# A sorted segment sum and three-layer MLP on TensorE: even edge groups summed into the accumulating bank, odd ones into a staging bank

## The chip, the cores and the metric

One core of a Trainium2 chip. The metric is the device time of one execution in microseconds (us), the median over the runs of a kernel. All durations below are from one profiled execution of the kernel before, whose own time stands beside the others.

## The reference, cut to what matters

```python
def _L0_gnn_ref(x, edge_attr, edge_index, W1, b1, W2, b2, W3, b3):
    agg_edge = jax.ops.segment_sum(edge_attr, edge_index[1], num_segments=12500)
    collected = jnp.concatenate([x, agg_edge], axis=1)
    h = jax.nn.silu(collected @ W1 + b1)
    h = jax.nn.silu(h @ W2 + b2)
    return x + h @ W3 + b3          # OUT_DIM is the whole of x here

h = jnp.maximum(_layernorm(x, axis=-1), 0.0)
x = x + _L0_gnn_ref(h, edge_attr_48, jnp.stack([src, dst]), W1, b1, W2, b2, W3, b3)
```

x is 12500 x 128, edge_attr_48 is 200000 x 48, both f32; `dst` is sorted. W1 is 176 x 256, W2 256 x 256, W3 256 x 128.

## The kernel before, in words

**Groups, windows, tiles.** The edges are cut into NG = 391 groups of 512 (128 partitions times PER = 4). As `dst` is sorted and a node has 16 edges on average, the 512 edges of a group reach nodes within a window of WINDOW = 42 columns. VectorE compares the edges' relative targets with the 42 columns (`onehot_of`, L628 to L635), TensorE multiplies a group's edges (128 x 48, stationary) by its one-hot (128 x 42, moving), four times, one for each j. That is the group's sum. A tile is 448 nodes and, on average, GPT = 14 groups; there are NT = 28 tiles. A batch is the 14 groups of a tile, in two halves of seven that are loaded and turned to one-hots apart.

**Two steps for a sum.** `sum_tile` (L919 to L944) takes the groups in pairs. The even group of a pair goes to partitions 0 to 47 of the PSUM bank `stage` and the odd one to partitions 64 to 111 of it, by the two column halves of the array (`tile_position` (0, 0) and (0, 64)), in turn; all addresses are constants. ScalarE copies `stage` to SBUF (`stage_sums`, L437). `place_batch` (L946 to L959) then multiplies each staged window by a slice of the identity, and adds it into one of the two banks of `agg_ps` at the window's offset. This offset is known on the chip only: `offsets_of` (L908 to L914) loads the 14 offsets of a batch from SBUF into registers of TensorE's sequencer. A tile's bank gets groups from up to EARLY = 3 before to 3 after its own, so the batch that is placed is shifted by three groups against the one that is summed (`batch_of`, L901). Every f32 matmul runs as two passes, each with a weight load, so a batch of 14 groups has 112 passes in the sum and 28 in the placement.

**The pipeline.** Each engine has a queue of its own, worked in order, with semaphores between them; the order is written out by hand in a function `step(i, parity)` for each engine, with i = 1 to 29, of which 4 to 21 are a loop of two steps a turn (`pipeline`, L258). On TensorE (L1019) step i is: `layer1(i-1)`, `offsets_of(i+1)`, `sum_tile(i+1)`, `layer3(i-2)`, `transposes(i)`, `place_batch(i+1)`, `layer2(i-1)`. On VectorE (L827): `add_x` (L801), `carry_over` (L763, reads the tile's bank and carries its 64 columns of overhang), `relu_lo`, `agg_lo`, a one-hot half, the statistics of x of tile i+1, `add_b3`, the low parts of h1, the other one-hot half, `shift_of_norm` and `finish(i-2)` (L819, waits for layer 3). On ScalarE (L506): `relu`, `split_agg` (L481), `clear_bank` (L418), `activate2(i-2)` (L487, its two halves free the banks that `layer1` writes), `activate1`, `normalize(i)`, `stage_sums(i+1)`. SyncE issues all loads and stores; the load of x of tile i+1 waits for `add_x(i-1)`.

**Ahead of the steps.** TensorE turns four sets of rows for the relative targets and offsets (`turn_rows`), sums batches 0 and 1, transposes tile 0, loads two sets of offsets, looks at a flag that sends bad data to a general path (`where_invalid`, L268), places both batches. ScalarE zeroes `agg_carry` in three pieces (`clear_carry`, L426) and splits the weights.

Of the kernel before, what the change touches and what calls it, by code (L numbers as in the profile page):

```python
# [33 lines left out]
def gnn_kernel(nc, x, dst, edge_attr, W1, b1, W2, b2, W3, b3, out):  # L34
# [33 lines left out]
    STAGED = PAIRS * WINDOW  # L68
    assert WINDOW <= OVER and FULL_ROWS == ROWS - 1
# [5 lines left out]
    def groups_of(i, half):  # L75
# [8 lines left out]
    with ExitStack() as ctx:  # L84
# [40 lines left out]
        offset_row = sb("offset_row", [1, NT * SLOT], I32)  # L125
# [160 lines left out]
        def _(sp):  # L286
# [5 lines left out]
            def load_edges(i, parity, half):  # L292
                n, full = groups_of(i, half)
# [3 lines left out]
                e0 = (i * GPT + half * HALF) * GROUP  # L297
                sp.dma_start(raw[:, slot, 0:full].rearrange("p g j d -> p g (j d)"),
                             edge_attr[bass.ds(e0, full * GROUP), :].rearrange(
# [66 lines left out]
            def step(i, parity):  # L366
                if has(i, -1, NT):
                    load_x(i + 1, 1 - parity)
                for half in range(2):
                    if has(i, -3, NT):  # L370
# [11 lines left out]
        def _(pool):  # L382
# [12 lines left out]
            pool.memset(w1e_lo[:, :].bitcast(F32), 0.0).then_inc(s_pool_zero, 1)  # L395
            pool.memset(agg_carry[:, 0:POOL_ZEROS], 0.0).then_inc(s_carry0, 1)
# [20 lines left out]
        def _(act):  # L417
# [19 lines left out]
            def stage_sums(t, parity):  # L437

                act.wait_ge(s_summed, 2 * t + 2)
                if not isinstance(t, int) or t > 1:  # L440
                    act.wait_ge(s_placed, t)
                act.activation(staged[:, parity].rearrange("d k w -> d (k w)"), stage[0:ROW2 + ED, 0:STAGED],
                               ACT.Copy).then_inc(s_staged, 1)
# [5 lines left out]
            rel_of(0)  # L449
            stage_sums(0, 0)  # L450
            clear_carry(1)
# [54 lines left out]
            def step(i, parity):  # L506
                if has(i, 1, NT):
                    relu(i - 1)
                if isinstance(i, int) and i == 1:
                    clear_carry(2)  # L510
# [19 lines left out]
        def _(dve):  # L530
# [97 lines left out]
            def onehot_of(i, parity, half):  # L628
                n, _ = groups_of(i, half)
                slot = 2 * parity + half  # L630
                cols = rel[:, :, :].rearrange("p g j -> p (g j)")[
                    :, bass.ds((i * GPT + half * HALF) * PER, n * PER)]
                return dve.tensor_tensor(onehot[:, slot, 0:n * PER, :],  # L633
                                         window[:, :].unsqueeze(1).broadcast_to([P, n * PER, WINDOW]),
                                         cols.unsqueeze(2).broadcast_to([P, n * PER, WINDOW]), ALU.is_equal)  # L635
# [7 lines left out]
            def weights_lo():  # L643
                dve.wait_ge(s_w_hi, 4)
                dve.wait_ge(s_pool_zero, 4)
# [10 lines left out]
            def offsets_into(b, first, last, many=1):  # L656
                g0 = b * GPT - EARLY + first
# [4 lines left out]
            FULL0 = (P + EARLY) // GPT  # L662
            REST0 = (P + EARLY) % GPT
            offsets_into(0, EARLY, GPT)
# [24 lines left out]
            offsets_into(FULL0 + 1, 0, GPT, NT - 2 - FULL0)  # L689
            offsets_into(NT - 1, 0, NG + EARLY - (NT - 1) * GPT)  # L690
            dve.tensor_reduce(any_invalid[:, :], invalid_sum, AX.X, ALU.max).then_inc(s_off, 1)
            weights_lo()
            dve.wait_ge(s_rel, ROWS)
            load_stats(1, 1)
            dve.wait_ge(s_stats, 2)
            aggregate_stats(1, 1)
            for half in range(2):
                make_onehot(2, 0, half)
            shift_of_norm(1, 1)

            def general_path():
# [25 lines left out]
                dve.wait_ge(s_pool_zero, 4)  # L727
# [5 lines left out]
                dve.wait_ge(s_onehot, 6)  # L733
# [29 lines left out]
            def carry_over(t, parity):  # L763

                n = PER * nodes_p(t)
                if isinstance(t, int) and t == NT - 1:
                    dve.wait_ge(s_placed, NT)
                else:
                    dve.wait_ge(s_closed, t + 1)
# [57 lines left out]
            def step(i, parity):  # L827
                if has(i, 1, NT):
                    add_x(i - 1, 1 - parity)
# [3 lines left out]
                if has(i, -2, NT):  # L833
# [21 lines left out]
        def _(pe):  # L855
# [45 lines left out]
            def batch_of(b):  # L901

                t = isinstance(b, int)
                first = 0 if t and b == 0 else -EARLY
                last = sum(groups_of(b, half)[0] for half in range(2)) if t and b == NT - 1 else GPT - EARLY
                return first, last

            def offsets_of(b):  # L908
                first, last = batch_of(b)
                _, offsets = nc.values_load_multi_w_load_instructions(  # L910
                    offset_row[0:1, bass.ds(b * SLOT + (first + EARLY), last - first)], engines=[mybir.EngineType.PE],
# [7 lines left out]
            def sum_tile(i, parity):  # L919

                counts = [groups_of(i, half) for half in range(2)]
                total = sum(n for n, _ in counts)
                wait(pe, s_staged, i)
                for pair in range(PAIRS):
                    for k in (2 * pair, 2 * pair + 1):
                        n, full = counts[k // HALF]
                        slot = 2 * parity + k // HALF
                        if k % HALF == 0:
                            pe.wait_ge(s_edges[slot], 16 * slot_turn(i, parity) + (16 if full < n else 0))
# [150 lines left out]
```

## Time and profile before

| | us |
|---|---|
| median of 3 runs | 358.68 (357.7 to 360.31) |
| the profiled execution | 358.91 |
| its span | 357.1 |
| around the span | 1.8 |
| granted TensorE clock, mean over the span | 0.981 of full speed |

PE is TensorE's matmuls, PEld its weight loads, PEldq its sequencer (registers, semaphores), DVE VectorE, ACT ScalarE. A row of a timeline has the start in us from the span's start, the duration in us, the engine, line and operation, and in brackets the idle time of the engine before it and what ended that.

### The profile page before, as it was taken

What the parts mean: (1) busy time and instruction counts of PE and PEld (TensorE: products, weight loads), DVE (VectorE), ACT (ScalarE), POOL (GpSimd) and SP (SyncE); (2) the same over time, 40 slices, a digit from 0 to 9 for tenths busy, and PEclk for the clock granted to TensorE, in tenths of its full rate; (3) what the DMA queues carried; (4) which work ended last, traced back from release to release, by engine and by line L of the source; (5) the groups of instructions that cost most, each with busy time, mean ns of one, the idle gap of its engine ahead of it and who ended that gap; (6) DMA issues with size and microseconds to landing.
All of it is one profiled execution on the core that took longest, in us unless ns stands there. A gap on an engine that the chain in (4) does not pass through costs nothing.

```text
span 357.1 us, 13469 instructions
## 1 busy us (share of the span) xinstructions
PE 326.2 (91%) x5150; PEld 296.9 (83%) x5151; DVE 266.5 (75%) x638; ACT 214.4 (60%) x406; POOL 42.4 (12%) x44
## 2 busy tenths in 40 slices
PE   6654999999999999999999999999999999999985
PEld 5643888988898888988898889888898889888984
DVE  7881968978877797778777787879777877776462
ACT  8452675557656675567555765667555755567471
POOL 3041101111001110111001110111011101111000
PEclk9986799999999999999999999999999999999999
DMA  6984057733675356634674357534763456512111
GB/s 196 303 219 149 21 163 209 207 117 106 195 206 154 99 157 206 191 108 119 199 206 135 100 176 206 175 103 133 205 206 110 125 181 207 163 33 52 28 28 49
DMA packets 79194, 53.07 MB, mean 149 GB/s; under 512 B 2912, under 2 KB 78778, under 8 KB 79168
## 3 DMA queue, kind: packets, MB, share of 16 engines
q1 hardware_dynamic: 79168, 52.70, 51.2%
q8 instruction: 19, 0.31, 0.4%
q14 instruction: 7, 0.06, 0.1%
HBM read 46.29 MB, written 6.40 MB: 148 GB/s over the span
## 4 chain that ended last, share of the span: by engine, by line
PE 87%; issue 5%; ACT 4%; DVE 3%; POOL 0%; ACTq 0%; POOLq 0%; DVEq 0%
PE stage L937 21%; PE z L1015 15%; PE agg_ps L954 11%; PE z L1000 8%; PE z L1004 6%; PE z L1001 6%; PE z L983 3%; PE z L988 3%; PE z L984 3%; PE z L989 3%; PE z L985 3%; PE tp L967 3%; ACT xn L471 1%; ACT agg_carry L428 1%; DVE g_tilet L545 1%
## 5 line engine op out<-in xcount | busy, mean ns | idle before, releaser
L937 PEld LDWEIGHTS stage<-onehot,raw 128*48 128x48 f32 x3128 | 73.9, 126 | 19.7 <-issue 19.5
L937 PE MATMUL stage<-onehot,raw 128*48 128x42 f32 x3128 | 77.0, 215 | 10.0 <-issue 9.1
L633 DVE TENSOR_TENSOR onehot<-window,rel 128x1176 f32<-128x1176 f32 (+1 forms) x56 | 76.9, 1376 | 1.9 <-ACT rel L434 1.2
L403 POOL TENSOR_TENSOR rstd<-vareps,minus_half 112x4 f32<-112x4 f32 (+1 forms) x28 | 39.2, 1401 | 287.1 <-DVE vareps L617 287.1
L1015 PE MATMUL z<-w,h 128*112 128x128 f32 (+1 forms) x448 | 56.3, 278 | 1.4 <-ACT h L492 0.8
L1015 PEld LDWEIGHTS z<-w,h 128*112 128x112 f32 (+1 forms) x448 | 50.6, 176 | 3.4 <-issue 2.1
L824 DVE TENSOR_TENSOR out_t<-z,resid 112x512 f32<-112x512 f32 (+1 forms) x28 | 19.3, 691 | 41.5 <-PE z L1015 41.5
L492 ACT ACTIVATE h<-z,b2c 128x448 f32<-128x448 f32 (+1 forms) x56 | 35.4, 632 | 21.5 <-PE z L1004 20.3
L954 PE MATMUL agg_ps<-staged,ident 112*48 112x42 f32 x782 | 42.5, 219 | 4.8 <-issue 4.8
L954 PEld LDWEIGHTS agg_ps<-staged,ident 112*48 112x48 f32 x782 | 39.2, 129 | 8.7 <-issue 5.0
L479 ACT ACTIVATE hT_hi<-tp 128x448 fp32r<-128x448 f32 (+1 forms) x28 | 15.2, 542 | 51.6 <-PE tp L967 51.6
L471 ACT ACTIVATE xn<-x_t,nmr,rstd 112x128 f32<-112x128 f32 (+1 forms) x112 | 45.8, 479 | 0.0
L1000 PE MATMUL z<-h_hi,w_hi 128*128 128x448 f32 (+1 forms) x112 | 43.8, 391 | 0.0
L500 ACT ACTIVATE h<-z,b1c 128x448 f32<-128x448 f32 (+1 forms) x56 | 35.0, 625 | 12.8 <-PE z L989 12.8
L1001 PE MATMUL z<-h_hi,w_lo 128*128 128x448 f32 (+1 forms) x112 | 40.9, 365 | 0.0
L607 DVE BATCH_NORM_STATS2 stats<-x_t 112x6 f32<-112x128 f32 (+1 forms) x112 | 24.4, 280 | 20.8 <-DMA x_t<-in_x_dram 20.7
L798 DVE TENSOR_TENSOR h_lo<-h,h_hi 128x448 fp32r<-128x448 f32 (+1 forms) x56 | 33.2, 622 | 7.2 <-ACT h_hi L504 6.9
L485 ACT ACTIVATE agg_hilo<-agg 48x448 fp32r<-48x448 f32 (+1 forms) x28 | 16.2, 578 | 34.7 <-DVE agg L774 34.6
L504 ACT ACTIVATE h_hi<-h 128x448 fp32r<-128x448 f32 (+1 forms) x56 | 32.3, 576 | 1.8
L1004 PE MATMUL z<-h_lo,w_hi 128*128 128x448 f32 (+1 forms) x112 | 31.9, 366 | 0.0
L1000 PEld LDWEIGHTS z<-h_hi,w_hi 128*128 128x128 f32 x112 | 21.0, 187 | 2.6
L1004 PEld LDWEIGHTS z<-h_lo,w_hi 128*128 128x128 f32 x112 | 21.0, 188 | 1.8
(107 smaller groups left out, 404.7 us busy)
## 6 DMA issues: line engine op xcount, KB each, us to landing
raw<-in_edge_attr_dram SPq DMA_DIRECT2D x55, 672.0 KB, 5.5
x_t<-in_x_dram SPq DMA_DIRECT2D x27, 224.0 KB, 3.5
out_dram<-out_t SPq DMA_DIRECT2D x27, 224.0 KB, 3.6
dst_rows<-in_dst_dram SPq DMA_DIRECT2D x1, 512.0 KB
raw<-in_edge_attr_dram SPq DMA_DIRECT2D x1, 480.0 KB, 4.9
dst_rows<-in_dst_dram SPq DMA_DIRECT2D x1, 256.0 KB, 2.7
out_t<-in_L_gnn_W_dram SPq DMA_DIRECT2D x1, 256.0 KB, 8.1
x_t<-in_x_dram SPq DMA_DIRECT2D x1, 192.0 KB
```

Of the source, the lines that this page charges most:

```text
L403: pool.tensor_tensor(rstd[0:np_, parity], vareps[0:np_, :], minus_half[0:np_, :], ALU.pow).then_inc(s_rstd, 1)
L471: ln = act.activation(xn[0:np_, parity, q, :], x_t[0:np_, parity, q, :], ACT.Identity, bias=nmr[0:np_, parity, q:q + 1], scale=rstd[0:np_, ...
L492: act.activation(h2[:, m, 0:n], z[:, m, 0:n], ACT.Silu, bias=b2c[:, m:m + 1]).then_inc(s_h2, 1)
L500: act.activation(h1[:, m, 0:n], z[:, m, 0:n], ACT.Silu, bias=b1c[:, m:m + 1]).then_inc(s_h1, 1)
L633: return dve.tensor_tensor(onehot[:, slot, 0:n * PER, :], window[:, :].unsqueeze(1).broadcast_to([P, n * PER, WINDOW]), cols.unsqueeze(2). ...
L798: dve.tensor_tensor(h1_lo[:, m, 0:n], h1[:, m, 0:n], h1_hi[:, m, 0:n].bitcast(F32), ALU.subtract).then_inc(s_h1_lo, 1)
L937: mm = pe.matmul(stage[at:at + ED, pair * WINDOW:(pair + 1) * WINDOW], raw[0:rows, 2 * parity + half, k, j, :], onehot[0:rows, 2 * parity ...
L954: mm = pe.matmul(banks[0:ED, bass.ds(offset, WINDOW)], ident[0:ROW2 + ED, at:at + ED], staged[:, parity if k >= 0 else 1 - parity, group / ...
L1000: pe.matmul(z[:, m, 0:n], w2_hi[:, k, cols], h1_hi[:, k, 0:n], start=(k == 0), stop=False)
L1001: pe.matmul(z[:, m, 0:n], w2_lo[:, k, cols], h1_hi[:, k, 0:n], start=False, stop=False)
L1004: mm = pe.matmul(z[:, m, 0:n], w2_hi[:, k, cols], h1_lo[:, k, 0:n], start=False, stop=(k == M - 1))
L1015: mm = pe.matmul(z3[0:np_, q, :], h2[:, k, q * np_:(q + 1) * np_], w3[:, k, :], start=(k == 0), stop=(k == M - 1))
```

## The change

Batches are shifted by SHIFT = 4 groups, for the sum as for the placement, so batch b is the groups 14b-4 to 14b+9, batch 0 has 10 groups, and there is a batch 28 of 3 groups (NB = 29). In a pair the even group is summed by its four matmuls straight into `agg_ps` at its offset, while the odd group goes to `stage` as before; only the odd ones are staged and placed, 7 a batch. `sum_tile` so waits for the clear bank and needs the offsets. TensorE's step is turned: `layer2(i-2)` stands first, with the load of the offsets of batch i+1 between its two halves m. ScalarE copies 48 partitions in place of 112; rows 0 to 63 of `staged` are zeroed once by GpSimd. Prologue: the offsets of batch 0 are loaded before its sum, batch 0 is placed early, those of batch 1 are loaded ahead of the small matmuls, the general path's flag is read before the transposes; ScalarE zeroes the second piece of `agg_carry` before it stages batch 0; VectorE moves the second half of one-hot 2, `shift_of_norm(1)` and `add_x(0)` behind the first `carry_over`, `relu_lo` and `agg_lo`. The last tile is normalized one step earlier.

```diff
     def groups_of(b, half):
-        g0 = i * GPT + half * HALF if isinstance(i, int) else 0
-        n = min(HALF, NG - g0)
-        return n, min(n, NG - 1 - g0)
+        g0 = b * GPT - SHIFT + half * HALF
+        if not isinstance(b, int):
+            return g0, 0, HALF, HALF
+        at = max(0, -g0)
+        n = max(0, min(HALF, NG - g0))
+        return g0 + at, at, n, min(n, max(at, NG - 1 - g0))
@@ stage_sums (ScalarE)
-                if not isinstance(t, int) or t > 1:
-                    act.wait_ge(s_placed, t)
-                act.activation(staged[:, parity]..., stage[0:ROW2 + ED, 0:STAGED],
+                wait(act, s_placed, t - 1)
+                act.activation(staged[ROW2:ROW2 + ED, parity]..., stage[ROW2:ROW2 + ED, 0:STAGED],
@@ ScalarE, ahead of the steps
+            clear_carry(1)
             stage_sums(0, 0)
-            clear_carry(1)
...
+            clear_carry(2)
+            normalize(0, 0)
             stage_sums(1, 1)
-            normalize(0, 0)
@@ step (ScalarE)
-                if has(i, 0, NT):
+                if has(i, 0, NT) and not (isinstance(i, int) and i == NT - 1):
                     normalize(i, parity)
-                if has(i, -1, NT):
+                if has(i, -1, NB):
                     stage_sums(i + 1, 1 - parity)
+                if isinstance(i, int) and i == NT - 2:
+                    normalize(i + 1, 1 - parity)
@@ VectorE, ahead of the steps
+            make_onehot(2, 0, 0)
             load_stats(1, 1)
             aggregate_stats(1, 1)
-            for half in range(2):
-                make_onehot(2, 0, half)
-            shift_of_norm(1, 1)
@@ step (VectorE)
+                    first = isinstance(i, int) and i == 1
+                    if not first:
+                        add_x(i - 1, 1 - parity)
                     carry_over(i - 1, 1 - parity)
                     relu_lo(i - 1)
                     agg_lo(i - 1)
+                    if first:
+                        make_onehot(2, 0, 1)
+                        shift_of_norm(1, 1)
+                        add_x(0, 0)
@@ sum_tile (TensorE)
+                first, last = batch_of(b)
+                wait(pe, s_staged, b)
+                wait(pe, s_clear, min(b + 1, NT) if isinstance(b, int) else b + 1)
+                for k in range(first, last, 2):
...
                     for j in range(PER):
+                        for side in range(min(2, last - k)):
...
+                            if side == 0:
+                                mm = pe.matmul(banks[0:ED, bass.ds(offsets[k - first], WINDOW)], edges, into,
+                                               start=False, stop=True, skip_group_check=True, tile_position=(0, 0))
+                            else:
+                                pair = k // 2
+                                mm = pe.matmul(stage[ROW2:ROW2 + ED, pair * WINDOW:(pair + 1) * WINDOW], edges, into,
+                                               start=(k == first and j == 0), stop=True, skip_group_check=True,
+                                               tile_position=(0, ROW2))
@@ place_batch (TensorE)
-                wait(pe, s_clear, b + 1)
-                for offset, k in zip(offsets, range(first, last)):
+                for k in odd:
...
+                    if k == min(odd[-1], 2 * EARLY - 1) and has(b, 1, NB):
                         mm.then_inc(s_closed, 1)
@@ layer2 (TensorE)
                 for m in range(M):
+                    if m > 0 and b is not None:
+                        offsets = offsets_of(b)
@@ step (TensorE)
+                if has(i, 2, NT):
+                    offsets = layer2(i - 2, i + 1 if has(i, -1, NB) else None)
+                elif has(i, -1, NB):
+                    offsets = offsets_of(i + 1)
                 if has(i, 1, NT):
                     layer1(i - 1)
-                if has(i, -1, NT):
-                    offsets = offsets_of(i + 1)
-                    sum_tile(i + 1, 1 - parity)
+                if has(i, -1, NB):
+                    sum_tile(i + 1, 1 - parity, offsets)
...
-                if has(i, 1, NT):
-                    layer2(i - 1)
@@ TensorE, ahead of the steps
-            sum_tile(0, 0)
             pe.wait_ge(s_off0, 1)
+            offsets = offsets_of(0)
+            sum_tile(0, 0, offsets)
             for c in range(1, ROWS):
                 turn_rows(c)
+            pe.wait_ge(s_pool_zero, 4)
+            place_batch(0, 0, offsets)
+            offsets = offsets_of(1)
...
-            sum_tile(1, 1)
+            sum_tile(1, 1, offsets)
+            where_invalid(pe, mybir.EngineType.PE, general_path)
             transposes(0, 0)
-            first_offsets = offsets_of(0)
-            offsets = offsets_of(1)
-            where_invalid(pe, mybir.EngineType.PE, general_path)
-            place_batch(0, 0, first_offsets)
             place_batch(1, 1, offsets)
```

## Rows read from the trace of the kernel before

**Rows 1.** The page: busy time of the engines, share of the span, instructions.
```profile
PE 326.2 (91%) x5150; PEld 296.9 (83%) x5151; DVE 266.5 (75%) x638; ACT 214.4 (60%) x406; POOL 42.4 (12%) x44
```
**Rows 2.** The chain that ended last, one steady step: start, us, what.
```profile
...
215.12 1.93 PE z L1015 x16
...
217.43 1.39 PE agg_ps L954 x28
...
223.48 0.44 issue
223.93 2.72 PE stage L937 x112
...
```
**Rows 3.** The timeline of the same step, all engines.
```profile
...
217.23 0.69 DVE L824 TENSOR_TENSOR out_t<-z,resid 112x512 f32<-112x512 f32 x1 [1.79 <-PE z L1015]
...
218.64 0.61 DVE L774 TENSOR_TENSOR agg<-agg_ps,agg_carry 48x448 f32<-48x448 f32 x1
...
219.28 0.58 ACT L485 ACTIVATE agg_hilo<-agg 48x448 fp32r<-48x448 f32 x1 [1.19 <-DVE agg L774]
...
219.76 0.58 ACT L419 ACTIVATE agg_ps<-zeros 48x512 f32<-48x512 f32 x1
...
220.28 0.62 ACT L492 ACTIVATE h<-z,b2c 128x448 f32<-128x448 f32 x1
...
221.08 0.19 PEld L983 LDWEIGHTS z<-hT_hi,w1x_hi 128*128 128x128 f32 x1
...
222.47 0.87 DVE L607 BATCH_NORM_STATS2 stats<-x_t 112x6 f32<-112x128 f32 x4 [0.50 <-DMA x_t<-in_x_dram]
...
223.12 0.36 PE L989 MATMUL z<-agg_hilo,w1e_lo 112*128 112x448 f32 x1
...
```
**Rows 4.** Line L910, whole span: duration ns min/median/max, first and last start.
```profile
L910 PEldq TENSOR_LOAD <-offset_row x28: 1113/1340/2829, 27.3 to 326.4; - x28
```
**Rows 5.** Line L954 from 32.5 to 33.8 us, the same columns.
```profile
L954 PEldq FUSED_REGOPS  x11: 37/37/37, 32.5 to 33.8; - x11
```
**Rows 6.** Line L930 from 223.6 to 224.7 us, the same columns.
```profile
L930 PEldq FUSED_REGOPS  x1: 48/48/48, 223.8 to 223.8; - x1
L930 PEldq ALU_OP  x1: 32/32/32, 224.6 to 224.6; - x1
```
**Rows 7.** The timeline of the prologue.
```profile
...
9.75 2.68 DVE L633 TENSOR_TENSOR onehot<-window,rel 128x1176 f32<-128x1176 f32 x2 [1.16 <-ACT rel L434]
...
14.56 4.30 ACT L428 ACTIVATE agg_carry<-zeros 48x4928 f32<-48x4928 f32 x1
...
22.23 0.14 DVE L691 TENSOR_REDUCE any_invalid<-z 1x1 int32<-1x2 f32 x1
...
24.95 2.67 DVE L633 TENSOR_TENSOR onehot<-window,rel 128x1176 f32<-128x1176 f32 x2
...
29.35 0.69 DVE L805 SCALAR_TENSOR_TENSOR resid<-xn,x_t 112x512 f32<-112x512 f32 x1 [0.67 <-issue]
...
32.64 4.22 PE L954 MATMUL agg_ps<-staged,ident 112*48 112x42 f32 x50 [4.78 <-issue]
35.62 0.62 DVE L774 TENSOR_TENSOR agg<-agg_ps,agg_carry 48x448 f32<-48x448 f32 x1 [5.57 <-PE agg_ps L954]
...
36.95 0.74 PE L983 MATMUL z<-hT_hi,w1x_hi 128*128 128x448 f32 x1
```
**Rows 8.** One stretch: length, busy us of each engine, granted clock, DMA share.
```profile
29.00:40.30 11.30, 7.57 (x59) 7.09 (x60) 5.28 (x11) 2.80 (x5) 0.00 (x0) 0.55 0.17 50
```
**Rows 9.** First matmul of layer1(1) and of layer1(25), from the timeline.
```profile
48.40 0.37 PE L983 MATMUL z<-hT_hi,w1x_hi 128*128 128x448 f32 x1
...
325.50 0.36 PE L983 MATMUL z<-hT_hi,w1x_hi 128*128 128x448 f32 x1
```
**Rows 10.** The page's DMA issues: KB each, median us to landing.
```profile
x_t<-in_x_dram SPq DMA_DIRECT2D x27, 224.0 KB, 3.5
```
**Rows 11.** The timeline of the last steps: transposes of the last tile.
```profile
341.91 0.56 PE L967 MATMUL tp<-ident,xn 101*128 101x101 f32 x4 [1.24 <-ACT xn L471]
```

More of the change, by code:

```diff
@@ L369, in step @@
                 for half in range(2):
-                    if has(i, -3, NT):
+                    if has(i, -3, NT) or has(i, -3, NB) and half == 0:
                         load_edges(i + 3, 1 - parity, half)
@@ L901, in batch_of @@
             def batch_of(b):
[L903 to L906, printed above, removed]
+                if not isinstance(b, int):
+                    return 0, GPT
+                return (SHIFT if b == 0 else 0), min(GPT, NG + SHIFT - b * GPT)
             def offsets_of(b):
@@ L917, in _ @@
             pe.wait_ge(s_clear, 2)
[L919 to L929, printed above, removed]
-                            pe.wait_ge(s_onehot, 2 * i + k // HALF + 1)
-                    for j in range(PER):
-                        for side in range(2):
-                            half, k = divmod(2 * pair + side, HALF)
-                            if 2 * pair + side < total:
-                                rows = P if k < counts[half][1] else TAIL_P
-                                at = ROW2 * side
-                                mm = pe.matmul(stage[at:at + ED, pair * WINDOW:(pair + 1) * WINDOW],
-                                               raw[0:rows, 2 * parity + half, k, j, :],
-                                               onehot[0:rows, 2 * parity + half, k * PER + j, :],
-                                               start=(pair == 0 and j == 0), stop=True, skip_group_check=True,
-                                               tile_position=(0, at))
-                                if 2 * pair + side == HALF - 1 and j == PER - 1:
-                                    mm.then_inc(s_summed, 1)
-                mm.then_inc(s_summed, 1)
@@ new lines, in sum_tile @@
+            def sum_tile(b, parity, offsets):
+                first, last = batch_of(b)
+                wait(pe, s_staged, b)
+                wait(pe, s_clear, min(b + 1, NT) if isinstance(b, int) else b + 1)
+                for k in range(first, last, 2):
+                    for half in range(2):
+                        if k <= half * HALF <= k + 1 or k == first and half == 0:
+                            if half * HALF < last:
+                                _, _, n, full = groups_of(b, half)
+                                slot = 2 * parity + half
+                                pe.wait_ge(s_edges[slot], 16 * slot_turn(b, parity) + (16 if full < n else 0))
+                                pe.wait_ge(s_onehot, 2 * b + half + 1)
+                    for j in range(PER):
+                        for side in range(min(2, last - k)):
+                            half, at = divmod(k + side, HALF)
+                            rows = P if at < groups_of(b, half)[3] else TAIL_P
+                            edges = raw[0:rows, 2 * parity + half, at, j, :]
+                            into = onehot[0:rows, 2 * parity + half, at * PER + j, :]
+                            if side == 0:
[6 more added lines that the diff above has]
+                                               tile_position=(0, ROW2))
+                            if k + side == HALF - 1 and j == PER - 1:
+                                mm.then_inc(s_summed, 1)
+                mm.then_inc(s_summed, 1 if last > HALF else 2)
@@ L946, in place_batch @@
             def place_batch(b, parity, offsets):
                 first, last = batch_of(b)
+                odd = range(first + 1, last, 2)
                 pe.wait_ge(s_staged, b + 1)
-                wait(pe, s_clear, b + 1)
-                for offset, k in zip(offsets, range(first, last)):
-                    group = k % GPT
-                    at = ROW2 * (group % 2)
-                    mm = pe.matmul(banks[0:ED, bass.ds(offset, WINDOW)], ident[0:ROW2 + ED, at:at + ED],
-                                   staged[:, parity if k >= 0 else 1 - parity, group // 2, :],
-                                   start=False, stop=True, skip_group_check=True)
-                    if k == EARLY - 1 and has(b, 1, NT):
+                for k in odd:
+                    mm = pe.matmul(banks[0:ED, bass.ds(offsets[k - first], WINDOW)], ident[0:ROW2 + ED, ROW2:ROW2 + ED],
+                                   staged[:, parity, k // 2, :], start=False, stop=True, skip_group_check=True)
+                    if k == min(odd[-1], 2 * EARLY - 1) and has(b, 1, NB):
```

72 lines of the change are left out of this document (37 added, 35 removed).

## The prediction, made before the changed kernel was run

> **What bounds the kernel now.** I read the page's busy shares first: TensorE is busy 91% of the span, VectorE 75% [rows 1]. Then the chain of waits. It is TensorE almost throughout, and a steady step shows its parts: the sum of a batch 2.72 us (112 passes, 24.3 ns each), layer 3 1.93, the placement 1.39 (28 passes, 49.5 ns each), layers 1 and 2, and 0.44 called issue ahead of each sum [rows 2]. The first matmul of layer1(1) starts at 48.40 and that of layer1(25) at 325.50, 24 steps later [rows 9]: 277.10 / 24 = 11.55 us a step. The issue gap is larger than the chain shows. The last matmul of layer 1 starts at 223.12 [rows 3], the first of the sum at 223.93 [rows 2]; layer 1's two sets of five start 2.04 us apart in all (221.08, weight load, to 223.12, matmul, of ten with 0.2 between), so about 0.2 of these 0.81 us is the matmul itself and 0.6 is idle. What fills it is the sequencer: it loads 14 offsets into registers, 1.34 us in the median [rows 4], and begins only when it has issued layer 1.
>
> **The placement.** Half of it goes: 14 of 28 passes at 49.5 ns, 0.69 us a step [rows 2]. The seven that remain still need the identity and the staged rows at the same sizes.
>
> **The sum.** The same 112 passes, in the same two column halves in turn, but half of them with a register address. The engine's rate I leave at 24.3 ns a pass [rows 2]. The sequencer is the question. In the placements 11 register steps lie between 32.5 and 33.8 us [rows 5], and this was right after a long gap, so the queue was empty: at most 0.13 us for a step with the four instructions of its matmul. Constant matmuls go out faster: between 223.8 and 224.6 the sequencer passed the 24 matmuls ahead of the wait for the second half, 0.03 us each [rows 6]. If the address of a group is worked out once for its four matmuls, a pair of groups costs the sequencer between 0.13 + 7 x 0.03 = 0.34 and, if register matmuls are dear in themselves, 4 x 0.10 + 4 x 0.03 = 0.52 us, against 8 x 2 x 24.3 = 0.39 of the engine. If it is worked out four times, 4 x 0.13 + 4 x 0.03 = 0.64. I take the first (nothing added), because the register step is an instruction of its own with a row of its own, 37 ns [rows 5], and one value can serve four matmuls; the bounds are 0 and 7 x 0.25 = 1.75 us a step.
>
> **The load of the offsets.** It now stands between the two halves of layer 2. Ahead of it are placement passes and the six matmuls of the first half, 6 x 0.2 = 1.2 us of queued work. With 1.34 us [rows 4] it is just about covered, and what sticks out falls into a wait that exists anyway (next part). So the 0.6 us of idle time goes. Bounds: the longest load took 2.83 us [rows 4], which would stick out by 1.5. The Trainium skill speaks against this step: "Runtime: NRT & Kernel Launch", Instruction fetch mechanics, gives about 200 ns for each register even in bulk. As an estimate from that page, 14 registers would be 2.8 us. The trace disagrees, with 1.34 in the median of 28 loads, and I go by the trace.
>
> **What is late next.** With 0.6 + 0.69 gone TensorE alone would need 11.55 - 1.29 = 10.26. But a loop through three engines holds it [rows 3]: after layer 3, VectorE writes out_t from 217.23, add_x, then agg from 218.64; ScalarE splits agg (219.28), clears the bank (219.76), and only then takes the first half of h2 (220.28 to 220.90). layer1 cannot start ahead of it, as it writes the bank that this reads; it started at 221.08. That margin was hidden by the placement. With it 0.69 shorter, layer1 starts at about 220.95: only 0.13 of the 0.69 is won there. 0.07 more is won at its second half, whose h2 is no longer late. Then the idle 0.6 goes in full. Step: 11.55 - 0.13 - 0.07 - 0.61 = 10.73. Over 24 steps 24 x 0.82 = 19.6 us. VectorE, at 266.5 / 28 = 9.5 of work a step [rows 1] and 0.50 of waiting for x [rows 3], needs 10.0, and fits. The new wait of the sum for the clear bank costs nothing: the clear ends at 220.34, three us before the sum [rows 3]. Neither does the smaller staging copy: its 294 columns stay.
>
> **The prologue.** TensorE stood idle 4.78 us for two loads, the flag and a branch [rows 7], and then ran to 40.3 at a mean granted clock of 0.55, about 1.2 GHz [rows 8]. Loads and flag now lie beside the one-hots and the normalization. What limits then is VectorE. One-hot 0 is shorter by 4 of 14 groups, 4/14 x 2.68 = 0.77 us [rows 7], and the small matmuls come earlier, since ScalarE's 4.30 us of zeros stand no longer ahead of the relative targets; so the check for invalid groups ends about 1.2 us earlier than at 22.4 [rows 7], held by GpSimd's first rstd. Then one one-hot half of two, 1.33 us, is taken out: the statistics are done at 24.95 + 1.33 - 1.2 = 25.1, the branch takes 0.67 [rows 7], the first carry_over starts at 25.8. From it to layer1(0) it was 36.95 - 35.62 = 1.33 [rows 7]: 27.15 in place of 36.95.
>
> Of these 9.8 us some is given back. VectorE still has the one-hot half (1.33) and add_x(0) (0.69) to do: after agg_lo (27.8) they end at 29.9. The load of x for tile 2 waits for this add_x, which stood at 29.35 before [rows 7], so it doesn't come earlier: 30.1 + 3.5 [rows 10] = 33.7. From the statistics to the next agg VectorE works 5.9 us (222.47 to 218.64 + 11.55, less 1.79 idle, rows 3), so agg(1) starts at 39.6 and layer1(1) at 39.6 + 1.33 = 40.95 in place of 48.40 [rows 9]: 7.5 won. Bounds: 10 if x comes in time, 5 if it or the weights land late or the clock stays low through sum 2. The pieces are in [rows 3, 7, 10].
>
> **The end.** A batch of three groups is added (about 0.4 to 0.7 us with its waits), the placement of batch 27 is halved (0.69), and the last tile is normalized before its transposes are due, which had waited 1.24 us [rows 11]. Together about 0.9 won.
>
> **The sum.** 7.5 + 19.6 + 0.9 = 28.0. The profiled execution took 358.9, with 357.1 of span; 358.9 - 28.0 = 330.9, and that execution is 0.2 above the median of 358.68, so the same number serves for the median: 331 us.
>
> **The rivals.**
>
> 1. The sequencer becomes the bound in the sum (the address is worked out for each matmul, or register matmuls are dear). For it: 0.52 to 0.64 us a pair against 0.39. It runs ahead of the engine by part of a us, which softens it: 0.4 to 1.3 a step, 0.8 in the middle, over 25 batches 20 us: 351. Against it: the step's own row, 37 ns. Chance 0.13.
>
> 2. The load of the offsets isn't hidden: it takes 2.8 us as the longest did [rows 4], or begins only when the first half of layer 2 has left the queue. layer1 then starts 0.9 to 1.0 late in each step, which gives back the steady gain, and 331 + 20 = 351. The page of the Trainium skill named above would have it so. Chance 0.05: a load that long is in the trace, but half of the 28 took 1.34 or less.
>
> 3. TensorE alone is the bound, because ScalarE's order leaves more room than I see: 10.3 a step, 24 x 0.43 = 10 less: 321. Against it: h2 ended at 220.90 and layer1 began at 221.08 [rows 3]. Chance 0.07.
>
> 4. The other side. The two column halves no longer run beside each other once one writes through a register into `agg_ps` and the other into `stage`. A pass then costs 49.5 ns, as in the placements, not 24.3 [rows 2]: 112 x 25.2 = 2.8 us more for each of 28 batches, 79 us, less the 28 won: 410. It decides from where a pass costs 28 us / (28 x 112) = 9 ns more, above 33 ns. Against it: array position, order and shapes are the same, and only the addresses differ. Chance 0.05.
>
> **How the numbers follow.** The forecast has 0.70, its own range is 323 to 340 (prologue 5 to 10 us, the loop 0.3 us a step either way). Rivals 1 and 2 reach to 351, rival 3 to 321. For 8 in 10 I take 321 to 346, which leaves out the far half of rivals 1 and 2 and all of rival 4. Within 1% (about what a measurement of this kernel can tell from no change) lies only the worst end of rivals 1 and 2: 0.04. Slower by over 1% is rival 4 and a little for a worst end of rival 1: 0.06. Faster by over 1%: 0.90.
>
> **What would show it.** Right: L954's successor has half the passes; the issue row ahead of the sum is gone; the sum takes 2.7 us; ScalarE's first h2 releases layer1 in each step, as a new wait of TensorE of 0.3 to 0.5 us; steps of 10.7; no idle stretch of 4.8 us in the prologue, and layer1(1) at about 41. Wrong: a sum over 3 us (rival 1; over 5, rival 4), a gap within layer 2 longer than 0.5 (rival 2), steps near 10.3 with no wait for h2 (rival 3), or VectorE waiting for nothing in the steady steps.

## The result, and the profile after

| | before | after |
|---|---|---|
| median, us | 359.47 (357.7 to 360.31, 4 runs) | 334.5 (332.06 to 335.19, 4 runs) |
| ratio to before, 95% interval | | 0.9291 [0.9261, 0.9321] |
| profiled execution / its span, us | 358.91 / 357.1 | 334.11 / 332.3 |
| granted TensorE clock, mean | 0.981 | 0.988 |
| layer1(0), layer1(1), layer1(25) start, us | 36.95, 48.40, 325.50 | 27.59, 41.43, 301.24 |
| mean step, layer1(2) to layer1(25), us | 11.56 | 10.77 |

The change saves 7.1%, 24.8 us of span. By the three marks of [rows 7, 9], 7.0 are won ahead of layer1(1), 17.3 in the 24 steps behind it (277.1 against 259.8), and 0.5 behind layer1(25).

The page of the changed kernel, busy time of the engines, answers to [rows 1]:

```profile
PE 311.3 (94%) x4758; PEld 276.8 (83%) x4759; DVE 267.2 (80%) x639; ACT 213.2 (64%) x407; POOL 42.3 (13%) x45
```

TensorE has 14.9 us less to do in 392 fewer passes, about half of the placement [rows 2]. The rest of the gain, 9.9 us, is time in which TensorE no longer stands idle. One steady step of it, from the timeline, answers to [rows 3] (start, us, engine, line, operation, in brackets the idle time ahead and its end):

```profile
200.56 0.69 DVE L827 TENSOR_TENSOR out_t<-z,resid 112x512 f32<-112x512 f32 x1
...
201.44 0.48 PE L1013 MATMUL z<-h_hi,w_hi 128*128 128x448 f32 x1
...
201.96 0.61 DVE L777 TENSOR_TENSOR agg<-agg_ps,agg_carry 48x448 f32<-48x448 f32 x1
...
202.56 0.19 PEld L1013 LDWEIGHTS z<-h_hi,w_hi 128*128 128x128 f32 x1
...
202.60 0.58 ACT L491 ACTIVATE agg_hilo<-agg 48x448 fp32r<-48x448 f32 x1 [1.18 <-DVE agg L777]
...
203.09 0.58 ACT L425 ACTIVATE agg_ps<-zeros 48x512 f32<-48x512 f32 x1
...
203.56 0.56 PE L1017 MATMUL z<-h_lo,w_hi 128*128 128x448 f32 x2
203.61 1.18 ACT L498 ACTIVATE h<-z,b2c 128x448 f32<-128x448 f32 x2
...
204.37 0.44 PE L993 MATMUL z<-hT_hi,w1x_hi 128*128 128x448 f32 x1 [0.25 <-ACT h L498]
...
204.65 0.36 PE L994 MATMUL z<-hT_hi,w1x_lo 128*128 128x448 f32 x1
...
206.29 0.37 PE L999 MATMUL z<-agg_hilo,w1e_lo 112*128 112x448 f32 x1
...
206.58 0.12 PEld L947 LDWEIGHTS agg_ps<-onehot,raw 128*48 128x48 f32 x1 [0.31 <-issue]
```

Three things are to be seen. The 0.81 us from the last matmul of layer 1 to the sum [rows 2, 3] are now 0.29 (206.29 to 206.58). Layer 2's last two matmuls take 0.2 each and so give way at 203.96, but layer 1 starts at 204.37: 0.4 us of idle time that was not there before. And that wait ends with ScalarE's h2, whose queue is agg's split, the clear of the bank, h2, back to back.

Two things of this step aren't the same in every step. The idle time ahead of layer 1, read off the same way, is 0.41 in one step and 0.19 in the next through the loop, 0.28 in the mean of layer1(3) to layer1(25). And here VectorE comes to out_t without waiting for layer 3, as it had waited 1.49 us for x 4.6 us before that; in 26 of the 28 steps it waits for layer 3, 1.1 us on average.

The register loads (line 918, over the span; then a load and the placement of this step: duration, and first and last start) answer to [rows 4, 5]:

```profile
L918 PEldq TENSOR_LOAD <-offset_row x29: 781/1345/1910, 9.3 to 308.6; - x29
...
L918 PEldq TENSOR_LOAD <-offset_row x1: 1338/1338/1338, 200.9 to 200.9; - x1
...
L964 PEldq FUSED_REGOPS  x7: 37/37/37, 199.2 to 200.0; - x7
...
L947 PEldq FUSED_REGOPS  x196: 37/37/42, 11.1 to 313.8; - x196
```

The load runs from 200.9 to 202.24. The sequencer reaches it 0.5 us before TensorE begins layer 2 (201.44), and it is over 0.3 us before the second half's first weights (202.56): hidden, with little to spare. Line 947 has 196 register steps for 196 even groups, so an address is worked out once for its four matmuls.

### The profile page after: what moved, and what is told of

Read it like the earlier page. It is cut to its first block, busy times and chain, and to the rows that moved or that the text cites. A ratio compares the mean times of both kernels' runs of the same rounds, so it can differ in the third digit from the quotient of the medians.

```text
span 332.3 us, 12657 instructions
## 1 busy us (share of the span) xinstructions
PE 311.3 (94%) x4758; PEld 276.8 (83%) x4759; DVE 267.2 (80%) x639; ACT 213.2 (64%) x407; POOL 42.3 (13%) x45
## 4 chain that ended last, share of the span: by engine, by line
PE 72%; DVE 10%; issue 8%; ACT 4%; POOL 2%; DMA 1%; DVEq 1%; SPq 0%; ACTq 0%; POOLq 0%
PE agg_ps L947 17%; PE z L1029 16%; PE z L1013 5%; PE z L993 5%; PE z L1014 4%; PE z L1017 4%; PE agg_ps L964 3%; PE z L994 3%; PE z L998 3%; PE z L995 3%; PE z L999 3%; PE stage L951 3%; DVE out_t L827 2%; ACT h L498 2%; DVE agg L777 2%
## 5 line engine op out<-in xcount | busy, mean ns | idle before, releaser
L947 PEld LDWEIGHTS agg_ps<-onehot,raw 128*48 128x48 f32 x1568 | 73.0, 125 | 10.7 <-issue 10.7
L947 PE MATMUL agg_ps<-onehot,raw 128*48 128x42 f32 x1568 | 76.9, 214 | 1.7 <-DVE onehot L639 1.7
L951 PEld LDWEIGHTS stage<-onehot,raw 128*48 128x48 f32 x1560 | 72.7, 125 | 0.1
L498 ACT ACTIVATE h<-z,b2c 128x448 f32<-128x448 f32 (+1 forms) x56 | 34.2, 624 | 4.9 <-PE z L1017 4.3
L993 PE MATMUL z<-hT_hi,w1x_hi 128*128 128x448 f32 (+1 forms) x56 | 23.4, 419 | 8.2 <-ACT h L498 4.6
L993 PEld LDWEIGHTS z<-hT_hi,w1x_hi 128*128 128x128 f32 x56 | 11.0, 196 | 17.6 <-issue 14.0
```

The source lines that it names most:

```text
L498: act.activation(h2[:, m, 0:n], z[:, m, 0:n], ACT.Silu, bias=b2c[:, m:m + 1]).then_inc(s_h2, 1)
L947: mm = pe.matmul(banks[0:ED, bass.ds(offsets[k - first], WINDOW)], edges, into, start=False, stop=True, skip_group_check=True, tile_positi ...
L951: mm = pe.matmul(stage[ROW2:ROW2 + ED, pair * WINDOW:(pair + 1) * WINDOW], edges, into, start=(k == first and j == 0), stop=True, skip_gro ...
L993: pe.matmul(z[:, m, 0:n], w1x_hi[:, cols], hT_hi[:, 0:n], start=True, stop=False)
```

## The experiments

Every step below is the mean from layer1(2) to layer1(25) in that kernel's profiled execution; ratios are to the kernel before, run beside it.

### Only the halved placement undone

All 14 groups staged and placed, the rest as changed.

```diff
-  mm = pe.matmul(banks[0:ED, bass.ds(offsets[k - first], WINDOW)], edges, into, start=False, ...)   # even
+  mm = pe.matmul(stage[0:ED, pair * WINDOW:(pair + 1) * WINDOW], edges, into, start=(k == first and j == 0), ...)
-  odd = range(first + 1, last, 2)
+  odd = range(first, last)
```

> The changed kernel with its first part undone: all 14 groups of a batch are summed into the staging bank at constant addresses and placed, the order of the steps and the early load of the offsets stay. Theory (the loop layer 3, out_t, agg, clear, h2, layer 1, sum sets the step): of the 0.70 us of placement that come back only 0.13 are felt, since TensorE waits for h2 anyway; with the slower sum (24.3 ns a pass in place of 22.5) a step is 10.75 + 0.13 + 0.2 = 11.1, the time 334.5 + 25 x 0.33 = 343. Rival (every pass of TensorE counts): step 10.75 + 0.70 + 0.2 = 11.65, time 357.

Measured: 353.7 us (353.21 to 354.07, 4 runs), ratio 0.985 [0.9833, 0.9867], step 11.57. Of the 25 us only 5 are left: the step is 0.5 over the theory's 11.1 and close to the rival's 11.65, yet not by the rival's road. Its trace says why (the timeline in layer 2; then the load and the register steps of the placement, as above; then a line of its waits, with us in total, times, longest us):

```profile
203.13 0.56 PE L1021 MATMUL z<-h_lo,w_hi 128*128 128x448 f32 x2
204.25 0.46 PE L1017 MATMUL z<-h_hi,w_hi 128*128 128x448 f32 x1 [0.55 <-issue]
```

```profile
L919 PEldq TENSOR_LOAD <-offset_row x1: 1886/1886/1886, 202.3 to 202.3; - x1
...
L968 PEldq FUSED_REGOPS  x14: 37/37/42, 199.2 to 201.4; - x14
```

```profile
PEld z L1017 <- issue: 15.7, 25, 1.0
```

Here the load starts at 202.3, when layer 2 already runs (202.22), and holds up its second half. Two things changed for the sequencer: it passes 14 placements with a register step each, and the load itself takes 1.89 us. Halving the placement thus did more than drop passes: it let the sequencer reach the load in time. My reading, to be tested, was that this run mixes two costs.

### The same with the load behind layer 2

```diff
 def layer2(t, b):
     for m in range(M):
-        if m > 0 and b is not None:
-            offsets = offsets_of(b)
         ...
+    if b is not None:
+        offsets = offsets_of(b)
```

> All groups staged and placed as in e1_all_placed, and the load of the offsets moved behind the second half of layer 2. In e1_all_placed the step came out at 11.57 where 11.1 was expected; its trace shows the load starting only when layer 2 was running and TensorE idle 0.55 us between the halves. Theory now: 14 register placements (0.115 us each on the sequencer, 0.099 on the engine) eat the sequencer's lead, so the load sticks out; with twelve matmuls ahead of it, it is covered, TensorE's own path is then 0.2 longer than the loop: step 10.95, time 339.5. Rival (the placement itself is felt in full, 0.70): step 11.4, time 350.

Measured: 340.68 us (338.67 to 340.87, 4 runs), 0.9468 [0.9429, 0.9506], step 10.99, with nearly every step 10.99. The load is as slow (1.91 us in the median), but covered. The chain of waits is TensorE alone, end to end across layer 2 and layer 1:

```profile
207.94 0.20 PE z L1016
208.14 0.40 PE z L1019 x2
208.54 0.20 PE z L997
```

So with the load covered the halved placement is worth 10.99 - 10.77 = 0.22 us a step, although it removes 0.6 of TensorE's time. The prediction had 0.20 for it.

This kernel sums nothing straight into `agg_ps`, and still it is 18.5 us faster than the kernel before beside it (359.21). So most of the 25 us comes from the turned step, the covered load and the prologue; the direct sum itself brings the last 6 (13 once the clear is moved, below).

### The load back in its old place

```diff
-    offsets = layer2(i - 2, i + 1 if has(i, -1, NB) else None)
+    layer2(i - 2, None)
     layer1(i - 1)
+    offsets = offsets_of(i + 1)
     sum_tile(i + 1, 1 - parity, offsets)
```

> The changed kernel with the load of the offsets back between layer 1 and the sum. Theory: the sequencer's 1.34 us is covered only by the layer 1 matmuls that are queued, and the sum starts 0.5 to 0.7 us later in each step, on the loop: step 11.35, time 334.5 + 26 x 0.6 = 350. Rival (the load was hidden anyway, the gain is all from the direct sum): 334.5 to 336.

Measured: 341.42 us (339.47 to 341.49, 5 runs), 0.9502 [0.9486, 0.9518], step 11.06. Between the two. The load costs 0.29 a step, half of the 0.6 I had given it. In this kernel layer 1 waits for h2 all the same (the timeline of TensorE, and the load):

```profile
207.59 0.44 PE L993 MATMUL z<-hT_hi,w1x_hi 128*128 128x448 f32 x1 [0.24 <-ACT h L498]
```

```profile
L918 PEldq TENSOR_LOAD <-offset_row x1: 1342/1342/1342, 208.2 to 208.2; - x1
...
L947 PEldq FUSED_REGOPS  x6: 37/37/42, 209.9 to 211.4; - x6
```

The load now ends 209.54, the sum's first register step is at 209.9, and layer 1 keeps TensorE until 209.6 (207.59 + 10 x 0.2). In this step the idle time is some 0.3. It alternates: where layer 1 has waited 0.41 for h2 the sum follows 0.5 behind the last matmul of layer 1, where it has waited 0.19 it follows 0.8 behind, as in the kernel before. In the changed kernel it is 0.29 in each, so over the 23 steps the load costs 0.29 and not 0.6.

### The early load alone, on the kernel before

The kernel before with the turned step and the load between the halves of layer 2; nothing else.

```diff
-    if has(i, 1, NT):
-        layer1(i - 1)
-    if has(i, -1, NT):
-        offsets = offsets_of(i + 1)
+    offsets = layer2(i - 2, i + 1 if has(i, -1, NT) else None)      # load between its halves
+    layer1(i - 1)
+    if has(i, -1, NT):
         sum_tile(i + 1, 1 - parity)
...
-    if has(i, 1, NT):
-        layer2(i - 1)
```

> The kernel before with one part of the change alone: TensorE's step turned and the offsets loaded between the halves of layer 2; 14 groups staged and placed, the prologue and the rest as before. Theory now: the gap ahead of the sum (0.6) goes, but a gap of 0.5 to 0.6 opens in layer 2, as in e1_all_placed: step 11.5, time 357 to 359. Rival (the early load is a gain of its own): step 10.95, time 344.

Measured: 361.81 us (360.8 to 362.5, 6 runs), 1.0065 [1.0044, 1.0086], step 11.65. No gain, a small loss, beyond the theory's range and 18 us from the rival. The gap ahead of the sum is gone (its first matmul now stands 0.29 us behind the last of layer 1, not 0.81) and stands in layer 2, 0.83 in one step and 0.34 in the next (the chain of waits):

```profile
210.82 0.41 PE z L1007 x2
211.24 0.83 issue
212.06 0.47 PE z L1003
...
223.35 0.34 issue
```

With the first run this shows that a load between the halves of layer 2 needs the halved placement ahead of it. Alone it moves an idle 0.6 us to another place. Behind layer 2 it is covered with all 14 placed as well (the run with the load moved there); that place wasn't tried on the kernel before.

### What holds layer 1: the clear behind h2

ScalarE's two instructions change places.

```diff
-    if has(i, 1, NT - 2):
-        act.wait_ge(s_carried, i)
-        clear_bank(1 - parity)
     if has(i, 2, NT):
         activate2(i - 2)
+    if has(i, 1, NT - 2):
+        act.wait_ge(s_carried, i)
+        clear_bank(1 - parity)
```

> The changed kernel with ScalarE's clear of the bank moved behind both halves of h2. Theory (the clear is in the loop): h2 is ready 0.57 us earlier, TensorE's wait ahead of layer 1 goes, and its own work is the bound: step 10.2 to 10.3, time 334.5 - 25 x 0.5 = 322. Rival (TensorE is already the bound and its wait is an artefact of the profile): step 10.75, 334.5.

Measured: 324.89 us (323.67 to 325.64, 4 runs), 0.9036 [0.9008, 0.9065], step 10.43, 17 of the 23 steps at 10.35 to 10.39. It beats both kernels, 2.9% below the changed one, and stands 2.9 us above the theory's 322. The timeline of a step shows h2 ahead of the clear and no wait left on layer 1:

```profile
197.09 0.58 ACT L491 ACTIVATE agg_hilo<-agg 48x448 fp32r<-48x448 f32 x1 [1.21 <-DVE agg L777]
...
197.58 0.62 ACT L498 ACTIVATE h<-z,b2c 128x448 f32<-128x448 f32 x1
...
198.42 0.37 PE L993 MATMUL z<-hT_hi,w1x_hi 128*128 128x448 f32 x1
...
199.15 0.58 ACT L425 ACTIVATE agg_ps<-zeros 48x512 f32<-48x512 f32 x1
```

TensorE alone is therefore 10.36 a step. The changed kernel adds the mean wait of 0.28 and, as the first matmul of layer 1 after a wait keeps TensorE 0.28 instead of 0.20 (204.37 to 204.65), another 0.08: 10.72 of its 10.77. The rest lies in a few longer steps.

Does the clear cost anything where TensorE has more to do? The same move on the kernel with all groups placed and the load behind layer 2:

> This is e5_all_placed_load_later (all 14 groups staged and placed, the load behind layer 2; 340.7 us, step 10.99 us) with ScalarE's clear of the bank moved behind its two halves of h2. Theory: with all placements in, TensorE alone is the bound of a step (its chain had no gap in e5) and layer 1 never waits for h2, so the move is worth nothing: 340 to 341 us, step 10.95 to 11.0. Then halving the placement and moving the clear are worth their 0.6 us a step only together (e3_clear_after_h2: 10.43). Rival: the order on ScalarE costs by itself, through h2 or the low parts, so the move wins some 0.2 to 0.35 us a step here as well, as it did in the changed kernel: 331 to 335 us.

Measured: 338.25 us (338.04 to 338.79, 4 runs), 0.943 [0.9404, 0.9455], step 11.00 against 10.99. In the steps the theory held: the move is worth nothing there and 0.34 in the changed kernel, and halving is worth 0.22 without it and 11.00 - 10.43 = 0.57 with it. The total came out below my range. The steps didn't do that: the second step took 11.08 in place of 12.56, which belongs to the section on the second step.

### The register address and the two column halves

The even groups at constant addresses, everything else as changed; so the sums of the even groups land in other columns than the reference's.

> The changed kernel with the even groups summed into the same bank at constant addresses (32 columns apart) in place of register addresses; the even groups' sums land in the wrong columns, all other work is the same. It tells why a pair of passes costs 45 ns in place of 48.6. If the cause is the separate banks of the two halves: still 45 ns, the same time within 1 us of 334. If it is the register address: 48.6 ns, step 0.2 longer, 339.

Measured once: 333.97 us, step 10.75, the sum's pace the same, 45 ns for two passes side by side. A register address costs nothing here that this measurement can see. The premise of a pace that had changed was wrong: the 24.3 ns a pass of the prediction [rows 2] had the end of the last matmul in it. From the first matmul of a sum to the first of layer 3 it is 2.65 us in this kernel, in the changed one and in the kernel before, and by the starts of the weight loads a pass takes 22.5 ns.

Both groups of a pair in one column half, so that nothing runs beside anything:

```diff
-    mm = pe.matmul(stage[ROW2:ROW2 + ED, ...], ..., tile_position=(0, ROW2))
+    mm = pe.matmul(stage[0:ED, ...], ..., tile_position=(0, 0))
```

> The changed kernel with the odd groups summed in the same column half as the even ones (partitions 0 to 47 of the staging bank), so that nothing runs beside anything. It prices the overlap of the two halves, which the prediction's fourth rival had as lost. Expected if the halves run beside each other in the changed kernel: a pass 45 to 49 ns in place of 22.5, 2.5 to 3.0 us more a batch, 334 + 28 x 2.75 = 411. If the overlap gives little: under 350.

Measured once: 395.53 us, step 13.26, 2.49 more. Two passes of one group now take 0.09 us (the chain):

```profile
203.31 0.09 PE agg_ps L948 x2
203.40 0.09 PE stage L952 x2
```

That is 45 ns a pass, against 22.5: 112 x 22.5 ns = 2.52, the measured 2.49. So the two halves do run beside each other in the changed kernel, and by this run rival 4 would have cost 61 us, not 79.

### The second step

From layer1(1) to layer1(2) the changed kernel takes 12.14 us, 1.4 more than I had. GpSimd's rstd(2) was the suspect (timeline of the changed kernel; then two stretches: length, busy us of PE, PEld, DVE, ACT, POOL with their instructions, granted clock, DMA share, GB/s):

```profile
35.00 1.15 DVE L801 TENSOR_TENSOR h_lo<-h,h_hi 128x448 fp32r<-128x448 f32 x2
36.07 1.37 DVE L639 TENSOR_TENSOR onehot<-window,rel 128x1176 f32<-128x1176 f32 x1
38.34 0.16 DVE L632 SCALAR_TENSOR_TENSOR nmr<-meanvar,rstd 112x4 f32<-112x4 f32 x1 [0.90 <-POOL rstd L409]
...
39.03 0.61 DVE L777 TENSOR_TENSOR agg<-agg_ps,agg_carry 48x448 f32<-48x448 f32 x1
...
41.43 0.71 PE L993 MATMUL z<-hT_hi,w1x_hi 128*128 128x448 f32 x1 [2.37 <-ACT h L498]
```

```profile
37.00:41.00 4.00, 1.61 (x7) 1.05 (x6) 3.04 (x8) 1.33 (x3) 1.31 (x1) 1.00 0.66 218
41.00:45.00 4.00, 3.57 (x10) 3.02 (x10) 3.35 (x12) 2.02 (x4) 0.55 (x1) 0.57 0.04 13
```

TensorE waits 2.37 us and then runs layer 1 at a granted 0.57 of full speed in the mean of that stretch, near the lower level of 1.2 GHz: matmuls start 0.37 us apart, not 0.20. The test puts the reader of rstd(2) ahead of the one-hot half:

```diff
+    if isinstance(i, int) and i == 1:
+        shift_of_norm(i + 1, 1 - parity)
     make_onehot(i + 2, parity, 1)
```

> The changed kernel with shift_of_norm(2) ahead of the second half of one-hot 3 in step 1. GpSimd's rstd of tile 2 took 3.14 us (1.0 to 1.4 in later steps) and ended 0.87 us after VectorE's one-hot; in the kernel before the one of 3.36 us ended 0.91 after the one-hots. Theory (GpSimd gets on only where VectorE pauses): rstd ends about 0.9 us after VectorE begins to wait, near 37.1, and takes 1.9 to 2.0 us; the time is the same within 1 us of 334, as VectorE waits earlier and no less. Rival (a first use, such as fetched code, makes it long): still 3.1 us, ending at 38.3, and VectorE's one-hot after it, so 1.4 us later in all.

Measured once: 333.76 us, layer1(1) at 41.18. The instruction itself comes close to what was expected (timeline of GpSimd and of VectorE; in the changed kernel the first took 3.14 us from 35.17):

```profile
34.92 1.85 POOL L409 TENSOR_TENSOR rstd<-vareps,minus_half 112x4 f32<-112x4 f32 x1 [8.61 <-DVE vareps L624]
```

```profile
36.80 0.16 DVE L632 SCALAR_TENSOR_TENSOR nmr<-meanvar,rstd 112x4 f32<-112x4 f32 x1 [0.90 <-POOL rstd L409]
36.88 1.38 DVE L639 TENSOR_TENSOR onehot<-window,rel 128x1176 f32<-128x1176 f32 x1
```

In both kernels rstd ends when VectorE has stood still for 0.90 us, however long it had been under way. Yet a pause of VectorE isn't needed in general: in the steady step shown first the same operation took 1.41 us beside the same two operations of VectorE, which didn't stop:

```profile
198.02 1.16 DVE L801 TENSOR_TENSOR h_lo<-h,h_hi 128x448 fp32r<-128x448 f32 x2
...
198.10 1.41 POOL L409 TENSOR_TENSOR rstd<-vareps,minus_half 112x4 f32<-112x4 f32 x1 [10.46 <-DVE vareps L624]
...
199.10 1.38 DVE L639 TENSOR_TENSOR onehot<-window,rel 128x1176 f32<-128x1176 f32 x1
```

So the order on VectorE changes how long rstd(2) takes, but why it is slow in that place and not in the steady steps stays open. For the time nothing is won: the one-hot half is then still to be done, so VectorE comes to add_x as late as before, and the second step takes 12.20. Both edits on one kernel:

> Both repairs on the changed kernel: the clear behind the two halves of h2 (e3_clear_after_h2, 324.9 us) and shift_of_norm(2) ahead of the one-hot half in step 1 (e8_rstd_wait_first). Theory: the second step, from layer1(1) to layer1(2), loses its wait for h2 and the low clock behind it, 0.8 to 1.3 us: 323.6 to 324.1 us, the steps after it unchanged at 10.4. Rival: in e3_clear_after_h2 that wait is already covered, or the one-hot half that is now later holds sum 3: 324.9 us or up to 1 us more.

Measured: 324.94 us (323.72 to 325.83, 4 runs), 0.9049 [0.9015, 0.9084], second step 11.92 against 11.93 with the clear alone. Nothing: the rival. What else is in that step is the clock. The kernel with the load back in its old place shows its price. There layer1(1) starts at 41.45 after a wait of 2.02 us for the same h2, so nearly as in the changed kernel, but at full clock (TensorE's first and last matmul of layer1(1), then its two stretches):

```profile
41.45 0.44 PE L993 MATMUL z<-hT_hi,w1x_hi 128*128 128x448 f32 x1 [2.02 <-ACT h L498]
...
43.36 0.37 PE L999 MATMUL z<-agg_hilo,w1e_lo 112*128 112x448 f32 x1
```

```profile
37.00:41.00 4.00, 2.43 (x12) 1.93 (x11) 3.04 (x7) 1.31 (x3) 1.33 (x1) 1.00 0.97 323
41.00:45.00 4.00, 3.55 (x70) 3.15 (x70) 3.93 (x12) 3.02 (x6) 0.46 (x1) 1.00 0.04 11
```

In the changed kernel the last matmul of layer1(1) is this one:

```profile
44.77 0.37 PE L999 MATMUL z<-agg_hilo,w1e_lo 112*128 112x448 f32 x1
```

From first to last the ten matmuls take 1.91 us there and 3.34 in the changed kernel, 1.43 more, and the second step takes 10.71 there and 12.14 here, also 1.43 more. So the whole loss of the second step is the low clock, and the wait for h2 ahead of it isn't by itself what costs it.

What brings the clock down isn't shown. In the kernel with all groups placed, the load behind layer 2 and the clear moved, TensorE worked 2.85 us of the stretch from 37 to 41, kept a granted 1.00 behind it, and the second step took 11.08. But without the clear moved it had worked 3.14 us there and still fell:

```profile
37.00:41.00 4.00, 3.14 (x21) 2.58 (x20) 3.07 (x7) 0.88 (x2) 1.77 (x1) 1.00 0.87 264
41.00:45.00 4.00, 3.12 (x14) 2.39 (x16) 3.90 (x13) 2.50 (x6) 0.10 (x1) 0.76 0.16 50
```

More work just ahead is therefore no safe sign. The low clock may also come in some executions of a kernel and not in others: one of the changed kernel's four took 332.06 us beside 334.11 to 335.19, and of the kernel with the load in its old place the profiled execution took 339.47 beside 341.13 to 341.49. Only one of each was profiled, so that isn't shown.

## Why the prediction was right or wrong

331 us was forecast and 334.5 measured, inside the forecast's own range of 323 to 340, and by its mechanism. In spans, 28.0 us were promised and 24.8 came. By its steps:

- **The loop, 19.6 us; 17.3 came.** The steady step was 10.77 against 10.73, which is 0.9 us over 23 steps. The other 1.4 us is the second step with its low clock. The prediction took all 24 steps for steady ones; this is the term that was mis-sized most. Its bounds do name a clock that stays low, but for the prologue.
- **The mechanism, "a loop through three engines holds it": shown.** The new wait for h2 was put at 0.3 to 0.5 us and is 0.28 in the mean, 0.41 and 0.19 in turn, so at the lower edge. Removing what lengthens that loop (the clear ahead of h2) gives 10.43. "TensorE alone would need 10.26" was nearly right too: 10.36. The step that rival 3 expected, 10.3, is that of the kernel one edit away.
- **The split of the step, -0.13 - 0.07 for the placement and -0.61 for the load: right as a way to the sum, wrong as prices of parts.** Undone alone, the halved placement costs 0.80 a step, the load's place 0.29; made alone on the kernel before, the load between the halves gains nothing. The prediction asked for the work queued ahead of the load, six matmuls of 0.2, "just about covered", and left out that this cover holds only because the sequencer has seven register steps fewer ahead of it and a load of 1.34, not 1.9. In the changed kernel the margin is 0.3 us in the step shown.
- **The sum, no change: shown**, 2.65 us before and after, at 22.5 ns a pass and not 24.3. An address is worked out once for a group, and constant addresses are no faster. Rival 1 falls. Whatever a register matmul costs the sequencer, it never held up the sum; that cost wasn't measured by itself.
- **Rival 2 (the load sticks out)** is what the two kernels with all groups placed and the load between the halves do: gaps of 0.55 and 0.83 us in layer 2, where it had 0.9 to 1.0. The Trainium skill's "Runtime: NRT & Kernel Launch", Instruction fetch mechanics, gives about 200 ns a register; the loads of 14 here took 1.34 us in the median, 0.10 each, and 1.91 at the slower place, 0.14 each. The measurements decide.
- **Rival 4:** priced by the run with one column half at 61 us, which would still have made the kernel slower.
- **The prologue, 7.5; 7.0 came.** layer1(0) was to start at 27.15 and did at 27.59, layer1(1) at 40.95 and did at 41.43. Between the two there is some luck: the way from layer1(0) to layer1(1) was to take 13.80 us and took 13.84, but by two errors that nearly cancel. agg(1) starts at 39.03, 0.6 earlier than the 39.6 of the sum, as x for tile 2 is there at 33.0 and not at 33.7. Then layer1(1) follows 2.40 behind it and not 1.33. The 1.33 was read at tile 0, which has no h2; here the clear and h2 stand ahead of layer 1 on ScalarE, the loop that the prediction names for the steady step and leaves out of the prologue. No run undid the prologue alone. Two kernels that both place all groups and load between the halves, one with the old prologue and one with the new, have layer1(1) at 49.85 and at 41.19.
- **The end, 0.9; 0.5 came.** Not taken apart.

What stays open: why one load takes 1.34 us and another 1.9. The slow ones are in the four kernels with all 14 groups placed and the load in or behind layer 2; the kernel before, also with 14 but with the load behind layer 1, has 1.34 [rows 4]. Open too are what brings the clock down in the second step, and why rstd(2) is slow there.

## What to carry to other kernels

When two edits of one step are read off a profile, price each with and without the other: whether a load is hidden depends on how far the sequencer runs ahead of its engine, and here seven more placements with a register step each were enough to lose that lead. When a bound engine is relieved, look at once for the wait that takes its place, and at what stands ahead of its releaser in that engine's queue: one instruction that nobody waits for yet, moved behind one that somebody does wait for, gave another 2.9% here.

## What was not expected of the hardware

- A small GpSimd operation (112 x 4) took very different times beside the same work of VectorE: rstd(2) took 3.14 us beside VectorE's h_lo and one-hot and 1.85 where VectorE stopped sooner, and in both cases it ended with VectorE's pause of 0.90 us. In the steady steps it took 1.18 or 1.41 beside h_lo and one-hot, with no pause at all.
- The same layer1(1), at nearly the same time and after nearly the same wait, ran at full clock in one kernel and near half of it in another, and that alone was worth 1.43 us.
- The same load of 14 registers took 1.34 us in some places and 1.9 in others, between kernels that differ in what stands ahead of it.
- A matmul whose output address comes from a register costs TensorE no more than one with a constant address (45 ns for two side by side, both), while on the sequencer the 14 register steps of a placement lie 2.2 us apart from first to last (199.2 to 201.4 in the first experiment), where the engine needs 1.39 for all of it [rows 2].
